# Counting edges by keys of a destination and half of the sources, 20 windows in place of 10 tiles

## The reference, cut to what matters

```python
xn = layernorm(x)
h = xn @ W; al = h @ a_l; ar = h @ a_r
e = exp(-leaky_relu(al[src] + ar[dst]))
h_prime = segment_sum(e[:, None] * h[dst], src) / (segment_sum(e, src) + 1e-5)
x = x + elu(h_prime) + mix(xn)      # mix: Fourier-feature attention, 16 heads, and a small MLP
x = x + bitlinear_ffn(layernorm(x))
```

## Time and profile before

| | us |
|---|---|
| median of 3 runs | 1246.85 (1245.67 to 1249.06) |
| the profiled execution | 1247.46 |
| its span in the trace | 1245.7 |
| PE busy in the span | 1187.0 (95%) |
| DVE, ACT, POOL busy | 757.5, 704.7, 337.1 |

### The profile page before, as it was taken

The page is one execution under the profiler, slowest core; times in us unless marked ns, Lnnn a source line. Parts: engine busy times, 40 slices in busy tenths (PEclk is TensorE's granted clock), DMA queues, the critical chain, the costliest instruction groups (busy, mean ns, idle before and its releaser), DMA issues. The chain is left out here.

```text
span 1245.7 us, 19482 instructions
## 1 busy us (share of the span) xinstructions
PE 1187.0 (95%) x6857; PEld 1040.2 (84%) x6857; DVE 757.5 (61%) x1248; ACT 704.7 (57%) x1070; POOL 337.1 (27%) x296
## 2 busy tenths in 40 slices
PE   6999998999999999999989999999989998999997
PEld 3555598999999999999978878999978877887884
DVE  7988815656665655665774676777753122556656
ACT  7265617777777777777786333322344332455543
POOL 1500013242414143333122010566635331211100
PEclk9999999999999999999999999999987999999999
DMA  8011140020201202020446566222253332712103
GB/s 221 11 21 29 32 96 1 1 71 0 71 21 50 63 8 71 0 71 0 138 126 215 165 194 203 77 87 87 76 184 99 99 80 71 218 33 66 30 6 99
DMA packets 72195, 99.41 MB, mean 80 GB/s; under 512 B 27242, under 2 KB 52166, under 8 KB 71632
## 3 DMA queue, kind: packets, MB, share of 16 engines
q1 hardware_dynamic: 68684, 86.11, 24.2%
q0 software_dynamic: 3456, 12.58, 3.4%
HBM read 77.04 MB, written 21.63 MB: 79 GB/s over the span
## 5 line engine op out<-in xcount | busy, mean ns | idle before, releaser
L1067 POOL TENSOR_TENSOR cos_sin_lo<-cos_sin,cos_sin_hi 125x1024 fp32r<-125x1024 f32 (+1 forms) x40 | 95.7, 2392 | 245.7 <-ACT cos_sin_hi L1179 245.7
L487 PE MATMUL p_cnt<-hot_s,hot_d 125*125 125x418 bf16 x540 | 113.7, 361 | 1.8 <-DVE hot_d L420 1.8
L418 DVE TENSOR_SCALAR hot_s<-iota_h,ends 125x1250 bf16<-125x1250 f16 x180 | 98.0, 544 | 14.5 <-PE p_cnt L487 12.5
L487 PEld LDWEIGHTS p_cnt<-hot_s,hot_d 125*125 125x125 bf16 x540 | 63.3, 139 | 51.5 <-DVE hot_d L420 40.5
L1571 PE MATMUL rows_in_psum<-x,mix_hi_v 128*128 128x416 f32 (+1 forms) x384 | 105.4, 356 | 0.0
L1571 PE MATMUL rows_in_psum<-x,mix_hi_q 128*128 128x416 f32 (+1 forms) x384 | 104.1, 352 | 0.0
L1571 PE MATMUL rows_in_psum<-x,mix_hi_k 128*128 128x416 f32 (+1 forms) x384 | 103.9, 351 | 0.0
L769 PE MATMUL rows_in_psum<-h_hi,a_lo 125*125 125x342 f32 x300 | 97.0, 323 | 5.9 <-POOL a_lo L611 3.8
L1675 PE MATMUL rows_in_psum<-x,xt_hi 128*125 128x512 f32 x320 | 100.4, 395 | 0.0
L769 PE MATMUL rows_in_psum<-h_hi,a_hi 125*125 125x342 f32 x300 | 96.4, 321 | 0.0
L769 PE MATMUL rows_in_psum<-h_lo,a_hi 125*125 125x342 f32 x300 | 96.4, 321 | 0.0
(11 more groups left out here) (310 smaller groups left out, 3091.3 us busy)
## 6 DMA issues: line engine op xcount, KB each, us to landing
x_in<-in_x_dram SPq DMA_DIRECT2D x30, 448.0 KB
attn_dram<-attn_t SPq DMA_DIRECT2D x8, 625.0 KB, 4.0
at_in<-attn_dram SPq DMA_DIRECT2D x10, 500.0 KB, 4.7
x_rows<-in_x_dram SPq DMA_DIRECT2D x10, 448.0 KB
x_in<-gnn_dram SPq DMA_DIRECT2D x10, 448.0 KB
out_dram<-rows SPq DMA_DIRECT2D x10, 448.0 KB
mix_in_v<-in_L_mix_wv_dram SPq DMA_DIRECT2D x8, 512.0 KB, 6.0
mix_in_k<-in_L_mix_wk_dram SPq DMA_DIRECT2D x8, 512.0 KB, 4.7
```

The costliest lines, as they stand in the source:

```text
L418: dve.tensor_scalar(hot_s[:, j, :], iota_h[:], ends[:, at, 0:1].rearrange("p a b -> p (a b)"), None, ALU.is_equal)
L487: last = pe.matmul(p_cnt[0:T, t % 2, n, 0:w], hot_d[:, j, 0:T], hot_s[:, j, a:a + w], start=False, stop=False)
L1067: pool.tensor_tensor(full(cs_lo, k), full(cs, k), f32(full(cs_hi, k)), ALU.subtract).then_inc(s_cslo[0], 1)
```

## The change

An edge gets a key, twice its destination plus 0 or 1 for the half of the sources in which its source lies (`part_of_s`), less a constant; its source becomes the offset within that half. A window is 125 keys (62.5 destinations, both halves) by 625 sources, and there are 20. `hot_s` shrinks from 1250 columns to 628, `hot_d` becomes `hot_k` with the same 125. A window fills two PSUM banks of 314 columns in place of three of 418 and 416; `p_cnt` still has two turns. Four DVE instructions on 250 columns per partition make keys and offsets at the start; POOL writes the table of keys (`iota_k`) in place of a DVE copy. `counts_dram` is laid out by destination: a stored row is now 1250 bytes of one piece (before, ten pieces of 250), a loaded tile of sources is ten pieces of 250 bytes per partition (before, one of 2500). `AFTER` turns one tile of x after each of the windows 3 to 12; before, two tiles of x came after the tiles 2 and 3. `normalise` of eight of the ten tiles of x moves in between.

```diff
+PARTS_OF_S = 2
+S_PART = -(-N // PARTS_OF_S)
+S_WIDTH = 628
+WINDOWS = NT * PARTS_OF_S
+BANK_PIECES = [(0, 314), (314, 314)]
+TURNS = 4 // len(BANK_PIECES)
-        hot_s = over_lo.put("hot_s", [T, HOT, N], BF16)
+        hot_s = over_lo.put("hot_s", [T, HOT, S_WIDTH], BF16)
-        AFTER = {0: (), 1: (0,), 2: (1, 2), 3: (3, 4), 4: (5,), 5: (6,), 6: (7,), 7: (8,), 8: (9,), 9: ()}
+        AFTER = {w: (w - 3,) if 3 <= w < 3 + NT else () for w in range(WINDOWS)}
+        FIRST_WINDOWS = 3
-            for t in range(NT):
+            for t in range(WINDOWS):
                 sp.wait_ge(s_kept, t + 1)
-                core.move(sp, core.counts_dram[:, :, t, :].rearrange("i p s -> p i s"), kept(t).rearrange("p (i s) -> p i s", i=NT),
-                          s_cst[t % 2])
+                core.move(sp, core.counts_of_keys[t * T:(t + 1) * T, :], kept(t), s_cst[t % 2])
-            keep_counts(0)
+            for t in range(FIRST_WINDOWS):
+                keep_counts(t)
             act.wait_ge(s_rstd, RSTD_STEPS)
-            for i in range(NT):
+            for i in range(2):
                 normalise(i)
-                if i == 3:
-                    keep_counts(1)
             act.wait_ge(s_gb, 1)
-            for t in range(2, NT):
+            for t in range(FIRST_WINDOWS, WINDOWS):
                 for i in AFTER[t - 1]:
+                    if i + 2 < NT:
+                        normalise(i + 2)
                     affine(i)
                 keep_counts(t)
...
+            split_step(dve.tensor_scalar(part_of_s[:], sources, float(S_PART), float(-KEY_SHIFT), ALU.is_ge, ALU.add))
+            split_step(dve.scalar_tensor_tensor(keys, keys, float(PARTS_OF_S), part_of_s[:], ALU.mult, ALU.add))
+            dve.tensor_reduce(bounds[:, 0, :], keys, AX.X, ALU.min).then_inc(s_efl, 1)
+            dve.tensor_reduce(bounds[:, 1, :], keys, AX.X, ALU.max).then_inc(s_efl, 1)
+            split_step(dve.scalar_tensor_tensor(sources, part_of_s[:], float(-S_PART), sources, ALU.mult, ALU.add))
+            split_step(dve.tensor_scalar(sources, sources, float(-S_PART * KEY_SHIFT), None, ALU.add))
...
-                            dve.tensor_scalar(hot_s[:, j, :], iota_h[:], ends[:, at, 0:1].rearrange("p a b -> p (a b)"), None,
+                            dve.tensor_scalar(hot_s[:, j, :], iota_s[:], ends[:, at, 0:1].rearrange("p a b -> p (a b)"), None,
                                               ALU.is_equal)
-                            dve.tensor_scalar(hot_d[:, j, 0:T], iota_t[:, t, 0:T], ends[:, at, 1:2].rearrange("p a b -> p (a b)"),
+                            dve.tensor_scalar(hot_k[:, j, 0:T], iota_k[:, t, 0:T], ends[:, at, 1:2].rearrange("p a b -> p (a b)"),
                                               None, ALU.is_equal).then_inc(s_hot, 1)
...
-                    for n, (a, w) in enumerate(THIRDS):
-                        pe.matmul(p_cnt[0:T, t % 2, n, 0:w], zeros[:], zero_rows[:, 0:w], start=True, stop=False)
+                    for n, (a, w) in enumerate(BANK_PIECES):
+                        pe.matmul(p_cnt[0:T, t % TURNS, n, 0:w], zeros[:], zero_rows[:, 0:w], start=True, stop=False)
...
             def load_counts(i):
-                core.move(sp, counts[:, i % SLOTS], core.counts_dram[i], s_cnt[i % SLOTS])
+                core.move(sp, counts[:, i % SLOTS], core.counts_of_sources[:, :, i * T:(i + 1) * T], s_cnt[i % SLOTS])
```

More of the change, by code:

```diff
@@ L364, in _, with split_step @@
             dve.wait_ge(s_efl, 1)
[L365 to L368, removed]
+            sources, keys = edges_f[:, 0], edges_f[:, 1]
+            split = [0]
+            def split_step(ins):
+                split[0] += 1
+                ins.then_inc(s_split, 1)
+                dve.wait_ge(s_split, split[0])
+            split_step(dve.tensor_scalar(part_of_s[:], sources, float(S_PART), float(-KEY_SHIFT), ALU.is_ge, ALU.add))
+            for n in range(2, PARTS_OF_S):
+                split_step(dve.scalar_tensor_tensor(part_of_s[:], sources, float(n * S_PART), part_of_s[:], ALU.is_ge, ALU.add))
+            split_step(dve.scalar_tensor_tensor(keys, keys, float(PARTS_OF_S), part_of_s[:], ALU.mult, ALU.add))
[3 more added lines that the diff above has]
+            split_step(dve.tensor_scalar(sources, sources, float(-S_PART * KEY_SHIFT), None, ALU.add))
             dve.wait_ge(s_tr, 1)
             dve.tensor_copy(row2[:].rearrange("p a (g c) -> p a g c", c=2),
-                            p_bound[0:NT, 0:4 * EDGE_ROWS].rearrange("p (a c g) -> p a g c", a=2, c=2)).then_inc(s_ends, 1)
+                            p_bound[0:WINDOWS, 0:4 * EDGE_ROWS].rearrange("p (a c g) -> p a g c", a=2, c=2)).then_inc(s_ends, 1)
             dve.wait_ge(s_pad, 1)
@@ L455, in _ @@
             for a in range(2):
-                last = pe.transpose(p_span[0:1, a * NT:(a + 1) * NT], span[:, a:a + 1], ident[0:NT, 0:NT])
+                last = pe.transpose(p_span[0:1, a * WINDOWS:(a + 1) * WINDOWS], span[:, a:a + 1], ident[0:WINDOWS, 0:WINDOWS])
             last.then_inc(s_spant, 1)
@@ L481, in count_tile @@
                     first, past = groups_of(pe, t, (r0, r1))
                     with pe.Fori(first, past, HOT):
-                        before = pe.snap(done, min_val=0, max_val=NT * (CHUNKS + HOT))
+                        before = pe.snap(done, min_val=0, max_val=WINDOWS * (CHUNKS + HOT))
                         for j in range(HOT):
                             pe.wait_ge(s_hot, before + j + 1)
-                            for n, (a, w) in enumerate(THIRDS):
-                                last = pe.matmul(p_cnt[0:T, t % 2, n, 0:w], hot_d[:, j, 0:T], hot_s[:, j, a:a + w], start=False, stop=False)
+                            for n, (a, w) in enumerate(BANK_PIECES):
+                                last = pe.matmul(p_cnt[0:T, t % TURNS, n, 0:w], hot_k[:, j, 0:T], hot_s[:, j, a:a + w], start=False, stop=False)
@@ L488, in count_tile @@
                             last.then_inc(s_used, 1)
                         pe.reg_add(done, done, HOT)
-                    for n, (a, w) in enumerate(THIRDS):
-                        last = pe.matmul(p_cnt[0:T, t % 2, n, 0:w], zeros[:], zero_rows[:, 0:w], start=False, stop=True)
+                    for n, (a, w) in enumerate(BANK_PIECES):
+                        last = pe.matmul(p_cnt[0:T, t % TURNS, n, 0:w], zeros[:], zero_rows[:, 0:w], start=False, stop=True)
                     last.then_inc(s_tile, 1)
-                count_tile(0)
+                count_window(0)
@@ L495, in _ @@
                 pe.wait_ge(core.vectors_loaded, 16 * len(COLUMNS))
                 pe.transpose(p_cols[:, 0:COLUMN_COUNT], core.vectors[:], ident[0:COLUMN_COUNT, 0:COLUMN_COUNT]).then_inc(s_vt, 1)
-                for t in range(1, NT):
-                    count_tile(t)
+                for t in range(1, WINDOWS):
+                    count_window(t)
                     for i in AFTER.get(t, ()):
@@ L1050, in _ @@
                     sp.wait_ge(s_tern, 2 * PIECES)
-                    core.move(sp, core.counts[:, 0], core.counts_dram[0], s_cnt0)
+                    core.move(sp, core.counts[:, 0], core.counts_of_sources[:, :, 0:T], s_cnt0)
                 for n in TERNARY_AT.get(i - 4, ()):
```

84 lines of the change are left out of this document (45 added, 39 removed).

## The result

The changed kernel takes 1230.60 us (median of 4 runs, 1229.59 to 1232.91) against 1246.53 us before (4 runs, 1245.67 to 1249.06): ratio 0.9871, 95% interval 0.9851 to 0.9891. It is 15.9 us faster; the forecast was 1231.5, 15.4 faster. The profiled execution took 1230.72 us, 16.7 less than the profiled one before; its span is 1228.9.

A forecast was written before the change was run, and what follows sets the result against it. DVE was taken to pace the first stage's count. Its barrier at 138.5 came 18.3 us earlier; less 1.5 (clock), 1.0 (slow jump) and 0.3 (loads), -15.5 us gave 1231.5 us, range 1226 to 1240.

The forecast's parts named there:

- The pass of 1.40: First stage's count: three chunks take 1.40 us start to start on DVE's sequencer, against 1.37 on the engine.
- Rival 2: First stage: none of the additions comes and the engine's 1.37 us a pass paces; 1227.5 us, chance 0.12.
- Rivals 4 and 5: First stage: PE at the lower clock for about half, 1240 us (0.12), or nearly all, 1250.5 us (0.04).
- Rival 3: First stage: the slow jump back is the rule, passes take 1.65 us; 1244 us, chance 0.07.
- Rival 6: Loads of counts are late: 2 to 5 us on top, 1235 us, chance 0.05.
- The start: Before the count: four DVE instructions for keys and offsets add 0.9 us (0.7 to 1.6); first chunk at 14.0.
- Windows 0 and 1: First stage: window 0 takes 18.2 us plus 0.5 and ends at 32.7; window 1 starts at 34.8, takes 8.4.
- term of 0.5 for a slow PE: Window 0: 0.5 us added because PE is still at its low clock.
- addition of 1.0 for single windows: First stage: 1.0 us added in case some windows have the jump back at 0.6 us instead of 0.35.
- Windows 4 to 14: Middle of the first stage: ACT's 5.8 us and the DVE and PE path's 6.2 alternate, 6.1 a window.
- addition of 1.5 for the clock: First stage: 1.5 us added for PE's lower clock after thin stretches, with PE busy some 60%.
- The end: End of the first stage: PE 0.8 us, the copy 0.85, then 1.47 to PE's next work, at 138.5.

The follow-up runs named there:

- r4: Changed kernel with DVE writing only 314 of the 628 columns of each one-hot of the sources: 1230.85 us in a single run.
- r6: Kernel before the change with only the new layout of the counts in memory: 1245.82 us against 1245.46, ratio 1.0001.
- r3: Changed kernel with sixteen tiny memsets ahead of DVE's count, shifting its code by 16 instructions: 1229.28 us, ratio 0.9857.
- r2: Changed kernel with POOL's table of keys written after DVE's conversion of the edges: 1230.23 us, ratio 0.9874.
- r11: Changed kernel with POOL's table of keys after DVE's conversion and sixteen memsets shifting DVE's code: 1228.61 us, ratio 0.9857.
- r1: Changed kernel run again with no edit: 1230.78 us, ratio 0.9882.
- r10: Changed kernel with POOL's table of keys after DVE's conversion and four `normalise`, not two, ahead of window 3's copy: 1227.84 us, ratio 0.9839.
- r12: Changed kernel with POOL's table late, sixteen memsets shifting DVE's code, and four `normalise` ahead of window 3's copy: 1225.29 us, ratio 0.9838.
- r9: Changed kernel with `keep_lo`, the subtraction leaving the low part of a tile of x, on POOL instead of DVE: 1233.32 us, ratio 0.9905.

## Why the prediction was right, and where its parts were not

**Right.** The pass of 1.40 set by DVE's sequencer (r4 shows it: another width, same pass); the 198 chunks; the window edge of 0.6; ACT and DVE in alternation, 5.9 a window; PE ahead of DVE except in window 0 and in the low spells of the clock; the loads of counts not late, and the layout neutral (r6). Rival 2 (the engine's 1.37 paces) is out, as a bare pass is 1.40. Rivals 4 and 5 (the low clock for half or nearly all of the stage) are out, as the clock stayed at 0.94 and more in each long stretch. Rival 3 (slow passes as the rule) is out, but true of window 1, of window 8 and of one pass in window 14 (r3). Rival 6 (late loads) is out. The Trainium skill's 512 bytes ("DMA: Bandwidth & Descriptors", Specifications) may hold for the rate of a transfer; here it did not show in the time, as the load stands ahead of its use.

**The start: +3.05, not +0.9.** The term itself was right: in r2 the first chunk is 0.58 later than before, with a conversion that is 0.32 shorter than the old 0.74, so 0.90 in all. What it left out is that POOL's work grew: the table of keys was costed at nothing, being "in place of a DVE copy". It is 2.5 us on POOL at the time of DVE's conversion, and the conversion waited for it and for the short writes behind it.

**Windows 0 and 1: 2.2 us too short.** From the first chunk to window 2's, the forecast had 29.8 and the trace has 31.97. Two different things make it up.

In window 0 it is PE. The first four passes took 1.55, 1.72, 1.56 and 1.70, 0.93 over four times 1.40. PE's matmuls of the products lasted 468 ns (median) there and 323 from 23 us on:

```profile
L514 PE MATMUL p_cnt<-hot_s,hot_k x9: 468/468/522, 18.7 to 20.9; 125*125 125x314 bf16 x9
...
L514 PE MATMUL p_cnt<-hot_s,hot_k x10: 298/323/348, 22.7 to 24.9; 125*125 125x314 bf16 x10
```

The slow passes end with the long matmuls in other executions too: in r2 the matmuls shorten near 18 us, and the fourth pass is 1.40; in r11 near 17, and the third is 1.41. This is the forecast's term of 0.5 for a slow PE, and it cost 0.93. The forecast put it down to the low clock; the granted clock reads 1.00 from 16 to 24 us, so only the lengths of the matmuls are shown, not their reason.

In window 1 it is mostly the place in the code: five passes and the edge cost 1.7 us over the forecast. The forecast had it as an addition of 1.0 for single windows. r2, with the clock at 1.00 there, has 1.95, 1.63, 1.61, 1.60 and 1.59; r11, with the code shifted, has 1.40 to 1.44. The changed kernel's 1.84 in place of 1.61 lies in its low spell. Windows 2 and 3 then ran at 1.40.

**Windows 4 to 14: close.** From the first `affine`'s end to the last one's 53.0 us (66.68 to 119.7), forecast 52.2 without its addition of 1.5 for the clock. In r1, without the low spell at 70 us, it is 52.2, so that spell cost 0.9. The one at 108 is in both; window 12 took 6.1 us with it and 5.6 in r10 and r12, where the clock stayed at 1.00, so it cost at most 0.5. With the 0.2 in window 1 the forecast's addition of 1.5 for the clock was of the right size. A copied piece takes 0.32 from start to start, not 0.37. The forecast's 6.1 a window is a slip in its own sum (5.8 and 6.2 alternating make 6.0).

**The end: as forecast.** From the last `affine` to PE's next work 24.6 us, forecast 24.1.

Together: 5.8 us later at the barrier than the 138.5 of the sum, of which 2.5 stood in the additions. That is 3.3 us less gain than forecast.

**Behind the barrier: 4.2 us that nothing in the forecast accounts for.** From the barrier to the end of the span the three profiles with the old count took 1088.9, 1088.1 and 1089.1 us. Eleven profiles with the new one took 1084.2 to 1089.8, mean 1086.3; both ends are kernels whose code behind the barrier is the same. So about 1.8 of the 4.2 is variation between executions (one stage takes 153.0 or 154.2 us in either program), and 2.4 is a difference of the means.

The profiles show where that difference lies. From PE's first work of line 2464 to that of line 2503 (2491 and 2530 in the changed kernel), near the end, the old three took 39.0 to 39.3 us and the new eleven 35.7 to 37.0. There ACT waits for a weight (`z` from `in_L_mix_w_dram`), and PE for what is made of it. Before:

```profile
1064.82 1.06 ACT L2196 ACTIVATE w_hi<-z 128x1024 fp32r<-128x1024 f32 x1 [2.51 <-DMA z<-in_L_mix_w_dram]
...
1067.84 0.50 PE L2492 MATMUL rows_in_psum<-w_hi,hidden_lo 128*125 128x512 f32 x1 [2.40 <-DVE hidden_lo L2361]
```

and after:

```profile
1049.11 1.06 ACT L2223 ACTIVATE w_hi<-z 128x1024 fp32r<-128x1024 f32 x1 [0.46 <-DMA z<-in_L_mix_w_dram]
...
1052.28 0.49 PE L2519 MATMUL rows_in_psum<-w_hi,hidden_lo 128*125 128x512 f32 x1 [0.48 <-DVE hidden_lo L2388]
```

In all three old profiles PE waits 2.4 to 2.6 us, and the granted clock of the ten microseconds around it is 0.83 (1064 to 1074 us above); in all eleven new ones it waits 0.5 to 1.3, and the clock there is 1.00 (1050 to 1060). The layout of counts is not the cause, as r6 waits 2.6. Why this weight lands earlier in the changed program, whose code is the same there, was not tested and stays open.

The closeness of 1231.5 to 1230.6 is thus partly luck: 3.3 us too much gain forecast before the barrier, and 4.2 us behind it forecast as nothing.

## What to carry to other kernels

When a loop's instructions get cheaper, read the sequencer's rows before the engine's: the loop of three chunks has a floor of 1.40 us, and a further halving of the width gave 2.1 us from the first chunk to the barrier in its one run (r4), before the passes that more windows would add. A change in granularity is only as good as the schedule that goes with it: the same 20 windows lose 12 us against the old kernel with the turns in pairs, and gain 16 with an even spread. Before an instruction goes to an idle POOL, look at what DVE does in that moment. Before a slow pass is put down to an edit, look at the granted clock of that microsecond, and at the lengths of PE's matmuls.

## What was not expected of the hardware

- A DVE instruction can be held for the whole of a POOL instruction beside it: a conversion of 0.42 us (r2) took 2.94 in the changed kernel, where it ended 0.03 before the last of four POOL writes that followed each other from 2.77 to 6.13 us, and 4.57 beside more writes of POOL (r4); a comparison of 0.37 took 1.85 beside a subtraction of 2.13 (r9). It seems to go the other way too: POOL's `minus_half` took 0.36 us beside the end of the conversion and 0.11 apart from it (rows at r2).
- DVE's passes are 0.2 to 0.6 us longer at places that go with the code's position (r3, r11), in part by a pause of its sequencer without a jump. The places are windows 1, 8 and 14, and one window earlier after a shift by 16 instructions, where window 1's is gone.
- PE's matmuls took 468 ns in place of 323 in window 0 while the granted clock read 1.00.
- Loads of 250-byte pieces cost nothing measurable where they are issued ahead of their use (r6, 1.0001).
